# Keys, values and their sums made feature-major in a one-core gated cross-attention and quantised feed-forward layer

## What is computed

```python
emb = layernorm(x) + ctx
q, k, v = emb @ wq + bq, emb @ wk + bk, emb @ wv + bv
mask = abs(i - j) < 64;  w = pos_bias * mask          # 512 x 512, the same for all batches
ek = exp(k - max_over_tokens(k));  ew = exp(w - max_over_keys(w))
num = einsum('tj,bjd->btd', ew, ek * v)
den = einsum('tj,bjd->btd', ew, ek)
attn = (sigmoid(q) * num / den) @ wo + bo
a = layer_norm(attn + emb)
r = layer_norm(relu(a @ w1 + b1) @ w2 + b2 + a)       # hidden width 1024
x = x + tanh(g_xattn) * r
# then: layernorm, int8-like rounding of tokens, ternary gate/up weights (1024 wide),
# silu(gate) * up, rounding again, ternary down weights, times tanh(g_ffn), plus x
```

## Time and profile before

| | us |
|---|---|
| median of three executions | 508.83 |
| lowest, highest | 508.54, 509.69 |
| span of the profiled execution | 507.9 |
| PE busy (matmuls) | 483.6 (95%) |
| DVE busy | 437.5 (86%) |
| ACT busy | 374.5 (74%) |
| POOL busy | 248.6 (49%) |

### The profile page before, as it was taken

One profiled execution on the slowest core, in us unless ns is written; L12 is line 12 of the kernel. 1 busy time (PEld: TensorE's weight loads), 2 busy tenths in 40 slices (PEclk: granted clock), 3 DMA queues, 4 the chain that ended last, 5 costly groups with the idle time before them and its releaser, 6 DMA issues.

```text
span 507.9 us, 9896 instructions
## 1 busy us (share of the span) xinstructions
PE 483.6 (95%) x3088; PEld 400.6 (79%) x3088; DVE 437.5 (86%) x1002; ACT 374.5 (74%) x611; POOL 248.6 (49%) x389
## 2 busy tenths in 40 slices
PE   8898999999999999999999999999999999999593
PEld 8686888988877987788877887788868887897352
DVE  6989988787989899898989799897899888957874
ACT  3583869867778778687878588686768687886874
POOL 7391364189125484248525484247415912656511
PEclk9997999999999999999999999999999999999789
DMA  5863251321112330222312430242113111330001
GB/s 185 184 216 122 43 203 47 62 62 57 53 21 43 97 94 21 43 63 72 95 23 62 84 92 13 43 63 73 53 25 80 65 22 21 63 84 3 21 22 42
DMA packets 64018, 34.72 MB, mean 68 GB/s; under 512 B 41696, under 2 KB 63456, under 8 KB 63968
## 3 DMA queue, kind: packets, MB, share of 16 engines
q1 hardware_dynamic: 63136, 34.09, 26.4%
q10 hardware_dynamic: 832, 0.00, 0.1%
HBM read 20.46 MB, written 4.19 MB: 49 GB/s over the span
## 4 chain that ended last, share of the span: by engine, by line
PE 76%; ACT 8%; DVE 6%; DMA 5%; issue 3%; POOL 1%; SPq 0%; DVEq 0%; ACTq 0%; POOLq 0%
PE ps L2516 47%; PE ps L2676 8%; PE ps L2576 7%; PE ps L2698 4%; DMA w_bit<-place_c 3%; PE ps L2585 3%; PE ps L2533 2%; DMA work<-in_L_xattn_wo_dram 2%; PE ps L2524 2%; DVE cols L1749 1%; PE ps L2593 1%; ACT place_c L1010 1%; DVE work L1743 1%; PE ps L2611 1%; ACT work L993 1%
## 5 line engine op out<-in xcount | busy, mean ns | idle before, releaser
L559 POOL TENSOR_TENSOR mv<-mv,cols 128x2 f32<-128x2 f32 x64 | 13.2, 206 | 162.6 <-DVE mv L1615 162.4
L2516 PE MATMUL ps<-w_hi,h_hi 128*128 128x256 f32 x256 | 75.9, 297 | 0.2
L2516 PE MATMUL ps<-w_lo,h_hi 128*128 128x256 f32 x256 | 71.5, 279 | 0.0
L2516 PE MATMUL ps<-w_hi,h_lo 128*128 128x256 f32 x256 | 71.4, 279 | 0.0
L942 ACT ACTIVATE h_hi<-ps,cols 128x512 fp32r<-128x512 f32 (+1 forms) x72 | 45.5, 637 | 13.6 <-PE ps L2516 8.6
L2516 PE MATMUL ps<-n1T_hi,w_hi 128*128 128x512 f32 (+1 forms) x144 | 54.1, 376 | 0.1
L1669 DVE RECIPROCAL ps<-ps 128x512 f32<-128x512 f32 x16 | 53.7, 3358 | 0.1
L2516 PE MATMUL ps<-n1T_lo,w_hi 128*128 128x512 f32 (+1 forms) x144 | 53.3, 370 | 0.0
L2516 PE MATMUL ps<-n1T_hi,w_lo 128*128 128x512 f32 (+1 forms) x144 | 53.2, 370 | 0.0
L2516 PEld LDWEIGHTS ps<-w_hi,h_hi 128*128 128x128 f32 x256 | 48.2, 188 | 3.3 <-DVE h_lo L1704 1.0
L988 ACT ACTIVATE work<-ps,cols 128x1024 f32<-128x1024 f32 x32 | 35.7, 1116 | 19.1 <-PE ps L2676 10.1
(11 more groups left out here) (186 smaller groups left out, 1493.0 us busy)
## 6 DMA issues: line engine op xcount, KB each, us to landing
x_in<-in_x_dram SPq DMA_DIRECT2D x16, 256.0 KB, 3.0
emb<-in_ctx_dram SPq DMA_DIRECT2D x16, 256.0 KB, 2.9
work<-in_x_dram SPq DMA_DIRECT2D x8, 512.0 KB, 3.7
out_dram<-work SPq DMA_DIRECT2D x16, 256.0 KB, 2.2
work<-in_L_xattn_w_dram SPq DMA_DIRECT2D x2, 1024.0 KB, 9.7
work<-in_L_ffn_w_gate_dram SPq DMA_DIRECT2D x1, 1024.0 KB, 5.5
work<-in_L_ffn_w_up_dram SPq DMA_DIRECT2D x1, 1024.0 KB, 5.6
place_c<-in_L_ffn_w_down_dram SPq DMA_DIRECT2D x1, 1024.0 KB, 7.6
```

The costliest lines, as they stand in the source:

```text
L2516: last = nc.tensor.matmul(dst, lhsT, rhs, start=(i == 0 and not begun), stop=(i == n - 1 and ends))
```

## The change

Keys and values are both computed with features on partitions, in full precision: `keys_T` grows from 4 to 12 matmuls of 512 columns, a new `values_T` has 12, `keys_values` goes. The bias of the keys and the negated maximum are now a column each, so that `exp_keys` takes exp(key - max) straight from PSUM as the bias operand of the activation, with `accum_out` giving the sum over the tile; it is called 8 times a batch on 128 columns (key tile and half) rather than 4 times on 256. `weighted` adds the value bias and multiplies in one instruction, again 8 times on 128 columns with `accum_out`. `max_row`, `bias`, `add_bias`, `key_sums`, `sum_lower` and two broadcast loads of bias rows go. The exponent and the product are then transposed by PE to tokens on partitions (`e_rows`, 4 transposes of 128x128 for each key tile, 16 a batch). The tile sums are staged by two small DVE instructions (`tile_sums`) and transposed once (`sums_T`); `attend_far` contracts 32 rows rather than 128. `far_weights` has one more instruction.

```diff
 def keys_T(b, h):
     wait(pe, embT_hi_ok, b, 2)
-    pe.wait_ge(hi_ok["wkv"], 1)
+    pe.wait_ge(lo_ok["wkv"], 1)
     bank_wait(b, "kT", h)
+    c = slice(h * P, (h + 1) * P)
     for k in range(ND):
-        last = nc.tensor.matmul(bank(b, "kT", h), wkv_hi[:, k, h * P:(h + 1) * P], embT_hi[:, k, :],
-                                start=(k == 0), stop=(k == ND - 1))
+        for i, w in enumerate((wkv_hi, wkv_lo)):
+            nc.tensor.matmul(bank(b, "kT", h), w[:, k, c], embT_hi[:, k, :], start=(k == 0 and i == 0), stop=False)
+    wait(pe, embT_lo_ok, b, 2)
+    for k in range(ND):
+        last = nc.tensor.matmul(bank(b, "kT", h), wkv_hi[:, k, c], embT_lo[:, k, :], start=False, stop=(k == ND - 1))
     last.then_inc(kT_ps.sem, 1)
+def values_T(b, h):
+    wait(pe, embT_lo_ok, b, 2)
+    ...
+    product(bank(b, "vT", h), [(wkv_hi[:, k, c], wkv_lo[:, k, c], embT_hi[:, k, :], embT_lo[:, k, :])
+                               for k in range(ND)]).then_inc(vT_ps.sem, 1)
-def max_row(b):
-    ...
-def keys_values(b, t):
-    ...
+def e_rows(b, j):
+    wait(pe, ekv_ok, b, ND * (j + 1))
+    bank_wait(b, "e", j)
+    c = slice(TILE[j] * P, (TILE[j] + 1) * P)
+    for i, e in enumerate((et, ev)):
+        for h in range(ND):
+            last = nc.tensor.transpose(bank(b, "e", j)[:, i * D + h * P:i * D + (h + 1) * P], e[:, h, c], ident[:])
+    last.then_inc(eT_ps.sem, 1)
-def key_sums(b):
-    ...
+def sums_T(b):
+    wait(pe, sums_lo_ok, b, 1)
+    bank_wait(b, "S")
+    nc.tensor.transpose(bank(b, "S")[:, 0:P], stage[:].bitcast(F32).rearrange("p g c -> p (g c)"), ident[:]).then_inc(s_ps.sem, 1)
 def attend_far(b, step, h):
-    nc.tensor.matmul(bank(b, step, h), esum[:, head(step, h)], far_w[:], start=False,
+    g = ND * (step == "den") + h
+    r = slice(32 * g, 32 * g + 32)
+    nc.tensor.matmul(bank(b, step, h), esum[r, :], far_w[r, :], start=False,
                      stop=True, skip_group_check=True).then_inc(...)
-def exp_keys(b, t):
-    wait(act, kvb_ok, b, t + 1)
-    nc.scalar.activation(bank(b, "kv", t)[:, 0:D], kv_f[:, t % 2, 0:D], ACT.Exp).then_inc(ek_ok.sem, 1)
+def exp_keys(b, j, h):
+    wait(act, nmx_ok, b, 1)
+    ...
+    nc.scalar.activation(et[:, h, c], bank(b, "kT", h)[:, c], ACT.Exp, bias=nmx[:, h:h + 1],
+                         accum_out=tsum[:, ND + h, j:j + 1]).then_inc(ek_ok.sem, 1)
+def neg_max(b):
+    nc.vector.tensor_tensor(mxb, mx, bk_col, ALU.add).then_inc(mxb_ok.sem, 1)
+    ...
+    nc.vector.tensor_tensor(nmx, bk_col, mxb, ALU.subtract).then_inc(nmx_ok.sem, 1)
-def bias(b): ...
-def add_bias(b, t): ...
-def weighted(b, t):
-    nc.vector.tensor_tensor(bank(b, "kv", t)[:, D:2 * D], bank(b, "kv", t)[:, 0:D], kv_f[:, t % 2, D:2 * D],
-                            ALU.mult).then_inc(ekv_ok.sem, 1)
+def weighted(b, j, h):
+    wait(dve, ek_ok, b, ND * j + h + 1)
+    wait(dve, vT_ps, b, h + 1)
+    ...
+    nc.vector.scalar_tensor_tensor(ev[:, h, c], bank(b, "vT", h)[:, c], bv_col[:, h:h + 1], et[:, h, c], ALU.add, ALU.mult,
+                                   accum_out=tsum[:, h, j:j + 1]).then_inc(ekv_ok.sem, 1)
-def sum_lower(b): ...
+def tile_sums(b): ...
```

More of the change, by code:

```diff
@@ L1797, in _ @@
+            far_masks()
             tile_stats(0, 0, 0)
             tile_stats(0, 0, 1)
+            tile_stats(0, 0, 2)
             mean_variance(0, 0, 0)
-            tile_stats(0, 0, 2)
             tile_stats(0, 0, 3)
             mean_variance(0, 0, 1)
+            position_max(0)
+            emb_lower(0, 0)
+            emb_lower(0, 1)
+            wkv_lower()
+            ewT_lower(0)
+            key_max(0, 0)
+            key_max(0, 1)
+            neg_max(0)
+            weighted(0, 0, 0)
@@ L1990, in _ @@
             tile_stats(2, 1, 3)
+            emb_lower(3, 1)
+            product(0, 0)
             mean_variance(2, 1, 1)
+            product_scale(0, 0)
+            key_max(3, 0)
             key_max(3, 1)
-            max_bias(3)
-            product(0, 0)
-            product_scale(0, 0)
-            bias(3)
+            neg_max(3)
             product(0, 1)
@@ L2235, in _ @@
             key_max(6, 0)
+            key_max(6, 1)
             product_scale(3, 0)
[L2237 to L2239 removed]
+            neg_max(6)
+            second_residual(4, 0)
+            second_residual(4, 1)
             product(3, 1)
[L2241 to L2244 removed]
             tile_stats(4, 2, 0)
```

2155 lines of the change are left out of this document (1084 added, 1071 removed), and 16 rows, old and new, of the table BANK.

## The result

Two measurements compare the changed kernel with the kernel before on the same chip. In the first, 20 executions of each: median 513.07 us after and 508.86 before, ratio 1.0063 [1.0044, 1.0082]. In the second, 10 against 25: 511.27 and 509.06 us, ratio 1.0038 [1.0001, 1.0075]. So the change makes the kernel 0.4 to 0.6% slower. The prediction was 505.4 us with slower at 0.22, range 497 to 512: wrong in direction. The time of the first measurement lies above the range, that of the second inside it; rival B, 511.2 us by the clock in the head, was the nearest case.

A forecast was written before the change was run, and what follows sets the result against it. PE was taken as the bound in settled batches, DVE as full as PE in the head. Span 507.9 - 7.6 (PE work) + 6.5 (head) - 2.8 (end) + 0.5 (table loads) = 504.5, with 0.9 505.4 us; range 497 to 512.

The forecast's parts named there:

- rival B: Head: new PE gaps lower the clock, slowing matmuls; head costs 11 us, kernel ends slower at 511.2 us; chance 0.20.
- Part 1: PE work in all batches: fewer matmuls against added transposes, net 0.94 us a batch saved, 7.6 us in all.
- the upper bound: PE work in all batches: 11.3 us saved if transpose runs cost nothing at their edges.
- the edges of a run: PE transposes: 0.15 us extra a run, some 3 runs of e_rows a batch.
- Part 2: DVE about 2 us a batch lighter, hidden in settled batches; ACT 0.7 to 2.3 more; 0.5 us in the sum for table loads.
- Part 3: First batches: a longer chain and later queries delay PE; 6.5 us of added idle PE taken, bounds 0 and 11.
- my upper bound: First batches: the head costs at most 11 us.
- The price of `neg_max`: Head: neg_max taken as 0.4 us in the chain before the first attend.
- The time that DVE's lighter load was to give back: Head, after the attention: DVE about 2.7 us lighter in batch 1, first hidden product 3.8 us late after attention 5.7 late.
- Part 4: End: work of batch 6 moves behind the last feed product into its waits; 2.8 us gained, between 0 and 4.
- Its sign: Rival B would show as a granted clock of 0.5 to 0.8 in the page's second and third slices.
- The 0.9 us: Whole kernel: the median of 508.8 us lies 0.9 us above the span of 507.9, added at the end.

The follow-up runs named there:

- e4: Changed kernel with attend_far on all 128 rows in place of 32, sums wrong: 504.99 us, ratio 0.9917 to the kernel before.
- e7: e5 with 40 more added matmuls, and attend_far on 128 rows with right sums by three more ScalarE copies a batch: 0.6 us gained by the latter.
- e5: Changed kernel with 62 added matmuls in three head waits, neg_max by columns, and position_max(1) moved behind weighted(0, 3, 1): 510.06 us.
- e12: e5 with far_row behind the queries, wq split earlier and e7's 128-row attend_far: 513.91 us.
- e13: Changed kernel with e9's fill, neg_max by columns, the second half's positions path moved ahead of the keys' chain, three banks swapped: 507.90 us, ratio 0.9980 to before.
- e15: e13 with wo_lower moved behind far_weights and another bank for positions_T(2): 505.49 us, ratio 0.9939 to the kernel before.
- e9: Changed kernel with 24 small matmuls added in the wait ahead of the first positions_T: 508.62 us.
- e17: Changed kernel with 62 small matmuls added in three waits of the head: 508.92 us.

## Why the prediction was wrong

**Part 1, PE work: right in kind, with a term missing.** The work fell by 10.8 us (the upper bound was 11.3). Transposes in a row start 0.11 us apart, four `e_rows` matmuls in 0.43. Where I took 0.15 us at the edges of a run there is nothing: over the five runs of `e_rows` in the middle that wait for nothing, the time from the matmul before to the second one behind is within 0.005 us of the sum of the steps. (In the row that I read it from, the 0.09 us behind the run is made up for by a last transpose that takes 0.03, which was already in my 0.103 us for each of eight; the 0.06 us ahead of it is not there at runs that wait for nothing.) The 32-row matmuls cost 4.6 us from 80 us on, where I had nothing in the sum. Net that would be about 6 us for 7.6. The marks agree: from the end of attention(0) to that of attention(7) the trace takes 366.5 us for 370.6, 4.1 less in seven batches, 0.6 a batch for the 0.94 forecast. (The loss of the middle grew by only 1.4 us, so some 3 us of other losses went; from what, no run shows.) The rule that I weighed from the Trainium skill (TensorEngine Tiling (Array Packing), Key Properties) was right: e4 and e7 show the edges. The same section says that different tiles can run matmuls in parallel; the pairs show that too.

**Part 2: right in the main.** `weighted` starts every 0.35 us, 2.8 us a batch (2.7 predicted). The table loads are 15, as counted. DVE is lighter by 8.6 us in all, not 16. Part of it went into operations held up beside POOL, which the part did not have: the steps of `neg_max` and `tile_sums` take 4.7 and 7.2 us over the eight batches, where at 0.16 and 0.17 to 0.18 us each they would take 2.6 and 2.8.

**Part 3, the head: this step failed.** By marks of the shorter group: `keys_T(0)` 17.92 (18.0 predicted), first attend 30.07 (28.4), attention through and `beta_w1` started 44.86 (43.0), first hidden 76.62 (72.8). The loss up to 80 us grew by 11.2 us, where the sum had 6.5: at my upper bound. Four things in it were wrong or missing.

- The price of `neg_max`: I had it at 0.4 us and it took 2.6 (21.68 to 24.24 us), most of the 1.7 us by which the first attend is later than forecast. I read each operation's price from other batches and counted list order, but never laid DVE's new list beside POOL's times, though POOL is busy 15.2 of 22 us there.
- The chain of the positions: I followed the keys' chain to the first attend and put no wait on the second. e5 and e12 show it, as 3.71 us ahead of `far_row` and 2.92 ahead of `positions_T`, and only with both chains moved does the time fall: by 0.7 us in e13, and by 2.4 more in e15, with `wo_lower` out of the way of `x_beta`.
- The time that DVE's lighter load was to give back: between the end of attention and the first hidden product I had 29.8 us (43.0 to 72.8). It is 31.8, the same as before the change (37.21 to 68.98 us), although DVE is busy 1.3 us less there (29.8 and 28.5 us). A lighter DVE did not shorten that stretch.
- The clock: part of the `e_rows` and attends of batch 0 run at 0.50 to 0.60. By e9 and e17 this is at most 1.8 us of the first hidden product's 7.6.

**Part 4, the end: right.** 3.3 us less loss for 2.8.

**Rival B's time came, only in part for its reason.** The longer group, two thirds of the executions, is what carries the median from 508.4 to 513 us. A fall of the clock in the wait ahead of `keys_T(0)`, which is B's mechanism, is seen in e4's trace, and with that wait filled the group is gone (e9). I gave B a fifth. Its sign, 0.5 to 0.8 in the second and third slices of the page, shows in the third (7 tenths) and not in the second. Its price was built otherwise: 5.6 us of slow matmuls for keys and values. The fall itself costs 1.3 us at `key_max`; the rest of the 4.0 us at the first attend comes from the POOL operations that `neg_max` (0.75 us) and `position_max(1)` (1.96) then meet. And against it I put that the clock was full in the gap before 16.18, but PE was idle for only 0.74 us there, and for 1.48 ahead of the transposes before it; the new wait is 2.69. That B's number, 511.2 us, lies near the median is luck, since the greater part of the head's cost stays with the clock at 1.00 (e9, e17).

**The time beside the span.** The 0.9 us were no such time. In every execution whose span is listed the time is 1.7 to 2.0 us above it, for both kernels; the span of 507.9 us fits the execution of 509.69, not the median. Since only the difference of 3.4 us was taken off, the sum comes to 505.4 either way. But the profiled execution before was a long one: by the medians the shorter group is 0.5 us under the kernel before, not the 1.2 of the spans.

**What stays open.** How many of the 20 longer executions have just e4's sequence can't be said from one trace of another kernel; the lower mean clock of 19 of them fits it. e4's own shorter executions, 502 to 505 us, have no trace. And the shares of the two chains and of the held-up operations in the head's cost were not measured one by one.

## To carry to other kernels

When a change makes the head's order new, lay the lists of VectorE and GpSimd side by side in time: an operation of 0.16 us with two SBUF inputs costs what is left of GpSimd's running one, here 2.31 us in all, and a small delay ahead of it can cost the whole next one. Moving one link of a head with two serial chains gives nothing until the other is moved as well; ask of each gain which wait ends last next. The wait of 2.69 us ahead of the first heavy matmuls was better filled, even with transposes of a constant. And read in a trace with the clock held how much of a delay the clock makes: here it was the smaller part.
